# An attention and mixture-of-experts kernel: three key/value groups per turn instead of two, with other pacing of the side work

## The chip, the cores and the metric

One Trainium2 chip, all eight cores, one program launched on all of them. The metric is the device time of the slowest core in microseconds (us). Each core works alone on half of the tokens of one batch element; no data passes between cores.

## The reference, cut to what matters

```python
# x: (4, 4096, 1024) f32, 16 heads of 64
qkv = einsum('btc,fc->btf', x, w_qkv)
p = softplus(q @ k.T * hs**-0.5) ** 2 * causal
attn = p / (p.sum(-1) + 1e-9)
x = layernorm(x + (attn @ v) @ w_proj.T + b_proj)
probs = softmax(x @ router_w.T); topk_vals, topk_idx = top_k(probs, 2)
topk_w = topk_vals / (topk_vals.sum(-1) + 1e-6)
out = sum over the 2 experts of (x @ expert_weights[e] + probs[e]) * topk_w[e]
x = layernorm(x + out)
```

## The kernel before, in words

A core owns 2048 query rows in four slots of 512; for slot 0 to 3 it attends to 1024, 2048, 3072 and 4096 keys. Heads are taken in eight head pairs. First all queries are projected (`qall`). Then comes the attention part, the subject here, and then a tail.

**Steps.** The list `seq` has 16 entries, called steps 0 to 15 here (`si` in the code): steps 0 to 7 are the eight head pairs in pass 0 (slots 0 and 1), steps 8 to 15 the same head pairs in pass 1 (slots 2 and 3).

**Turns.** A step runs over pairs of 128-key blocks: 4 + 8 = 12 turns in a step of pass 0, 12 + 16 = 28 in one of pass 1, 320 in all. They are numbered from 0 within a step. In turn n the program issues, in this order:

1. TensorE: four score matmuls into `psS`, which is one set of four banks. They wait for the Exp of turn n-1, which reads it.
2. `pop_av` (L432): the probability-times-value matmuls (AV) of turn n-2. When that was the last turn of a slot, four VectorE copies take `psA` and `psB` out; that happens in turn 1 and in turn 5 (pass 0) or 13 (pass 1). After the last slot of a step, so in turn 1 of the next, `queue_epilogue` (L463) queues nine items.
3. Groups of the keys and values of the step after this (`kv_groups`, L287): 20 groups in four chunks of 512 tokens, each chunk one K group (8 matmuls of 512 columns) and four V groups (8 of 128 columns). Groups use the banks `psK` and `psV` in turn (`bg_bank`, L275), and each is copied out by VectorE before its bank is used again. Turn 0 of a step has no groups. The chunks' inputs lie in two buffers `xkb`: when the last V group of a chunk is issued, the load of the chunk after the next is put into GpSimd's queue (1 MB, `load_xk`). Once no group is left, the call that finds none issues what the step after the next one needs: its weights `wqK` (0.5 MB) and two `xkb` chunks (1 MB each).
4. One item of the epilogue `epi_q`: turn 1 adds 1e-9 (VectorE), turns 2 and 3 a reciprocal each (VectorE), turns 4 to 7 one store `scr` each (2 KB to HBM, GpSimd's queue), turns 8 and 9 one broadcast load `bcb` (two DMAs of 64 KB, GpSimd's queue) and the VectorE product `attn<-attn,bcb`. A `bcb` load waits for all four `scr` stores of the step; the product waits for `bcb`.
5. In pass 1, after the 72 epilogue items of pass 0, items of `work_q`: projection, layernorm, routing and expert matmuls for the first half of the rows. An item has a tag: 1 holds matmuls, 2 holds VectorE or ScalarE work, 0 neither. At most one item of tag 1 or 2 goes into a turn. Tag 0 are the expert weight loads (256 KB each, four to a half of an expert, GpSimd's queue), issued in the four turns before the half is needed. What is left of `work_q` goes to the tail.
6. ScalarE: Exp (`t_exp<-psS`) and Ln (`spb<-t_exp`). There is one `spb`, so Ln of turn n waits until VectorE has squared that of turn n-1.
7. VectorE: the square `pbb<-spb`, and in the last four turns of a slot the mask product `pbb<-pbb,mkb`.

Every engine runs its own instructions in the order of issue. All loads of `xkb`, `wqK` and expert weights, and `scr` and `bcb`, go through GpSimd's one DMA queue; SyncE's queue has the spill of keys and values to HBM (`kvs`, 1 MB after group 20 in pass 0) and the residual rows `stream` (4 MB, at the start of step 2, and 4 MB more in the tail).

In the profile every instruction has line 1066, that of the helper that emits it, so groups are told apart by tile names.

Of the kernel before, what the change touches and what calls it, by code (L numbers as in the profile page):

```python
# [24 lines left out]
PASS_SLOTS = {0: (0, 1), 1: (2, 3)}  # L25
# [39 lines left out]
def build_program(debug=DEBUG):  # L65
# [75 lines left out]
    with contextlib.ExitStack() as ctx:  # L141
# [52 lines left out]
        def load_wq_usage(k, guard_t):  # L194
            hp = k % 8
            qn = "WQ%d" % (k % 4 if k < 8 else k % 2)
            wts = [(sem["T"], guard_t)] if guard_t else []
            if k < 8:
                dst = wqA[k % 4]
                src = ap(d_wq8, hp * D * 384,  # L200
                         [[384, 128], [384 * 128, 8], [1, 384]])
            else:
                dst = wqK[k % 2]
                src = ap(d_wq8, hp * D * 384 + 128,
                         [[384, 128], [384 * 128, 8], [1, 256]])
            ld_wq[k] = (qn, emit("g", "dma_start", dst, src,
                                 w=wts, i=[(qn, 16)]))
# [10 lines left out]
        def load_xk(p, hp, tc):  # L218
            bi = tc % 2
            qn = "XB%d" % bi  # L220
            wts = [(sem["T"], xkb_guard[bi])] if xkb_guard[bi] else []
            xk_load[(p, hp, tc)] = (qn, emit(
                "g", "dma_start", xkb[bi],
                ap(d_xkf, 512 * tc, [[4096, 128], [4096 * 128, 8], [1, 512]]),
                w=wts, i=[(qn, 16)]))
# [178 lines left out]
        v_cool = [0]  # L404
# [483 lines left out]
        for si, (hp, p) in enumerate(seq):  # L888
# [19 lines left out]
            for slot in PASS_SLOTS[p]:  # L908
                npair = PAIRS[slot]
                for j in range(npair):  # L910
# [23 lines left out]
                    if len(av_queue) >= 2:  # L934
                        pop_av()
                    if not (slot == PASS_SLOTS[p][0] and j == 0):
                        for _ in range(2):
                            ng = next(kvq, None)
                            if ng is not None:
                                ng()  # L940
                            elif not kv_done[0]:
                                kv_done[0] = True
                                if si + 2 < len(seq):
                                    load_wq_usage(8 + si + 2,
                                                  kv_tlast[seq[si]])
                                    nhp, npp = seq[si + 2]
                                    for tc in ((0, 1) if npp == 0 else (4, 5)):
                                        if (npp, nhp, tc) not in xk_load:
                                            load_xk(npp, nhp, tc)
                    v_cool[0] = max(0, v_cool[0] - 1)  # L950
                    heavy_done = 0
                    pops = 0
                    if slot == PASS_SLOTS[p][1] and j >= npair - 1:
                        heavy_done = 1
                    if epi_q:
                        epi_q.pop(0)()
# [1 line left out]
                    while (work_q and pops < 3  # L958
                           and epi_pops[0] >= P0_EPI):
                        tag = work_q[0][0]  # L960
                        if tag == 1 and heavy_done:
                            break
                        if tag == 2 and (heavy_done or v_cool[0]):
                            break
                        fn = work_q.pop(0)[1]
                        fn()
                        pops += 1
                        if tag:
                            heavy_done = 1
                        if tag == 2:  # L970
                            v_cool[0] = 1
                    par = gpair[0] % 2
                    gpair[0] += 1
                    wexp = [(sem["T"], t_sc)]
# [173 lines left out]
```

How the kernel before makes its waits and increments, by code:

```python
            def run(eng):  # L1058
                for waits, method, args, kw, incs in recs[key]:
                    for s, val in waits:
                        if val:
                            eng.wait_ge(s, val)
                    if method == "wait_ge":
                        eng.wait_ge(*args)
                        continue
                    instr = getattr(eng, method)(*args, **kw)
                    for nm, n in incs:
                        instr.then_inc(sem[nm], n)
```

## Time and profile before

| | before |
|---|---|
| median of the runs | 2041.87 us (2 runs, 2040.83 to 2042.9) |
| the profiled execution | 2041.92 us; its slowest core's span 2040.2 us (core 3) |
| spans of the eight cores | 2009.8 to 2040.2 us |
| query projection, up to the first Exp | 0 to 140.5 us |
| steps 0 to 7 | 140.5 to 591.1 us |
| steps 8 to 15 | 591.1 to 1646 us |
| tail | 1646 to 2040 us |

Busy time of an engine over the whole span says little here, since the stages have different limits; what is read is how far apart the Exp activations of successive turns lie, and what ScalarE waited for in between.

### The profile page before, as it was taken

The page shows a single profiled execution, that of the slowest core. Times are in us where ns is not written, and L with a number is a line of the kernel's source. Part 1 is how long each engine was busy: PE and PEld are TensorE (multiplying, and loading weights), DVE is VectorE, ACT ScalarE, POOL GpSimd, SP SyncE. Part 2 cuts the span into 40 slices and gives each one's busy share as a digit, 9 for nine tenths or more (in the row PEclk, how much of TensorE's full clock was granted, in tenths as well). Part 3 has the DMA queues.
Part 4 walks back from the last instruction along what each step waited for, and adds up shares of the span by engine and source line. Part 5 has one row for each costly group of instructions (what it writes and reads, how often), then busy time and mean ns, then how long its engine had stood idle before and what let it go on. Part 6 is the DMA issues. An engine that isn't in the chain of part 4 may idle for free.

```text
span 2040.2 us, 26095 instructions; the slowest of 8 cores (2009.8 to 2040.2 us)
## 1 busy us (share of the span) xinstructions
PE 1456.4 (71%) x7968; PEld 638.4 (31%) x7968; DVE 1155.7 (57%) x1524; ACT 1234.5 (61%) x687; POOL 245.5 (12%) x362
## 2 busy tenths in 40 slices
PE   1967666666777785758887887688884436599991
PEld 0433333333333232323433333234331112344440
DVE  0026757777666666655666555456667437444446
ACT  0229867888887979969788696597897720000000
POOL 1000111111111010020110200201100001022110
PEclk9978887888898989889999999899996758599995
DMA  9888677876875033281471833714300023144542
GB/s 159 111 120 129 106 154 127 127 114 105 139 119 79 1 66 55 42 119 22 81 101 28 114 57 59 107 22 81 50 1 6 0 72 119 22 77 70 82 63 82
DMA packets 146384, 162.47 MB, mean 80 GB/s; under 512 B 8784, under 2 KB 135888, under 8 KB 146128
## 3 DMA queue, kind: packets, MB, share of 16 engines
q0 software_dynamic: 137328, 128.10, 44.1%
q1 hardware_dynamic: 8928, 32.71, 4.4%
q8 instruction: 75, 1.23, 0.2%
q14 instruction: 53, 0.43, 0.1%
HBM read 269.65 MB, written 16.97 MB: 140 GB/s over the span
## 4 chain that ended last, share of the span: by engine, by line
PE 32%; ACT 28%; DMA 17%; DVE 11%; issue 10%; POOL 1%; DVEq 1%; ACTq 0%; SPq 0%; POOLq 0%
ACT spb L1066 14%; ACT t_exp L1066 14%; PE psK L1066 13%; PE psV L1066 11%; DMA xkb<-xkf 6%; PE psS L1066 4%; DVE pbb L1066 3%; DMA qall<-ew 3%; PE psA L1066 2%; DMA bcb<-scr 2%; DMA xq<-xqf 2%; PE psB L1066 2%; DMA scr<-rsb 2%; DVE rsb L1066 2%; DVE stream L1066 2%
## 5 line engine op out<-in xcount | busy, mean ns | idle before, releaser
L1066 ACT ACTIVATE t_exp<-psS 128x2048 bf16<-128x2048 f32 x320 | 600.7, 1877 | 225.2 <-PE psS L1066 202.5
L1066 ACT ACTIVATE spb<-t_exp 128x2048 bf16<-128x2048 bf16 x320 | 611.2, 1910 | 83.9 <-DVE pbb L1066 41.7
L1066 DVE TENSOR_TENSOR pbb<-spb 128x2048 bf16<-128x2048 bf16 x320 | 390.1, 1219 | 270.8 <-ACT spb L1066 254.1
L1066 PE MATMUL psS<-qall,kb 64*128 64x512 bf16 x1280 | 211.4, 408 | 217.8 <-ACT t_exp L1066 195.9
L1066 PE MATMUL psA<-pbb,vb 128*65 128x512 bf16 x640 | 272.2, 425 | 78.4 <-DVE vb L1066 31.3
L1066 PE MATMUL psB<-pbb,vb 128*65 128x512 bf16 x640 | 268.8, 420 | 0.0
L1066 ACT ACTIVATE lnr<-lnv 128x4 f32<-128x4 f32 (+1 forms) x6 | 1.2, 206 | 365.0 <-DVE lnv L1066 365.0
L1066 DVE SCALAR_TENSOR_TENSOR stream<-psK,gates,stream 128x512 f32<-128x512 f32 x128 | 95.8, 748 | 144.2 <-PE psK L1066 143.8
L1066 PE MATMUL psK<-qall,h1fm 128*128 128x512 bf16 x512 | 128.0, 395 | 53.4 <-DMA qall<-ew 39.8
L1066 DVE TENSOR_TENSOR pbb<-pbb,mkb 128x2048 bf16<-128x2048 bf16 x128 | 156.8, 1225 | 13.4 <-DVE pbb L1066 0.2
L1066 PEld LDWEIGHTS psA<-pbb,vb 128*65 128x65 bf16 x640 | 74.5, 116 | 275.1 <-issue 246.4
L1066 DVE SCALAR_TENSOR_TENSOR stream<-psV,gates,stream 128x512 f32<-128x512 f32 x128 | 95.7, 748 | 103.6 <-PE psV L1066 103.2
L1066 PEld LDWEIGHTS psS<-qall,kb 64*128 64x128 bf16 x1280 | 43.2, 95 | 339.5 <-issue 337.2
L1066 POOL DMA_DIRECT2D xkb<-xkf x64 | 57.3, 897 | 745.2 <-PE psK L1066 438.2
L1066 PE MATMUL psV<-qall,h1fm 128*128 128x512 bf16 x512 | 124.0, 386 | 12.5 <-DVE kb L1066 6.7
L1066 PE MATMUL psK<-ewh,h1fm 128*128 128x512 bf16 x512 | 122.6, 383 | 6.4 <-DVE g_t L1066 6.4
L1066 PE MATMUL psV<-ewh,h1fm 128*128 128x512 bf16 x512 | 121.2, 380 | 0.0
L1066 DVE CAST kb<-psK 128x512 bf16<-128x512 f32 x32 | 22.1, 692 | 160.6 <-PE psK L1066 160.3
L1066 PE MATMUL psK<-xkb,wqK 128*128 128x512 bf16 x256 | 77.9, 459 | 31.4 <-DMA xkb<-xkf 22.6
L1066 PE MATMUL psS<-xq,wqA 128*128 128x512 bf16 x256 | 62.2, 407 | 45.5 <-DMA xq<-xqf 41.5
L1066 PEld LDWEIGHTS psB<-pbb,vb 128*65 128x65 bf16 x640 | 76.3, 119 | 40.5 <-issue 12.3
L1066 PEld LDWEIGHTS psK<-qall,h1fm 128*128 128x128 bf16 x512 | 50.2, 100 | 116.9 <-issue 64.8
(90 smaller groups left out, 1421.7 us busy)
## 6 DMA issues: line engine op xcount, KB each, us to landing
xkb<-xkf POOLq DMA_DIRECT2D x64, 1024.0 KB, 11.9
qall<-ew POOLq DMA_DIRECT2D x64, 256.0 KB, 7.3
ewh<-ew POOLq DMA_DIRECT2D x64, 256.0 KB, 6.0
wqK<-wq POOLq DMA_DIRECT2D x16, 512.0 KB, 8.3
stream<-xot SPq DMA_DIRECT2D x16, 512.0 KB, 11.4
wqA<-wq POOLq DMA_DIRECT2D x8, 768.0 KB, 20.9
out<-stream SPq DMA_DIRECT2D x12, 512.0 KB, 2.6
kvs<-vb SPq DMA_DIRECT2D x8, 520.0 KB, 11.0
```

Source lines behind the costliest of these rows:

```text
L1066: instr = getattr(eng, method)(*args, **kw)
```

## The change

Three constants in the loop over turns. Up to three groups are issued in a turn instead of two. The last two turns of a step, not only the last one, take no item of tag 1 or 2. After an item of tag 2 the counter `v_cool` is set to 2 instead of 1; it is lowered by one ahead of the test, so a 1 never held anything back, and a 2 holds back a tag 2 item (and what stands behind it) for one turn.

```diff
@@ -934,7 +934,7 @@
                     if len(av_queue) >= 2:
                         pop_av()
                     if not (slot == PASS_SLOTS[p][0] and j == 0):
-                        for _ in range(2):
+                        for _ in range(3):
                             ng = next(kvq, None)
                             if ng is not None:
                                 ng()
@@ -950,7 +950,7 @@
                     v_cool[0] = max(0, v_cool[0] - 1)
                     heavy_done = 0
                     pops = 0
-                    if slot == PASS_SLOTS[p][1] and j >= npair - 1:
+                    if slot == PASS_SLOTS[p][1] and j >= npair - 2:
                         heavy_done = 1
                     if epi_q:
                         epi_q.pop(0)()
@@ -968,7 +968,7 @@
                         if tag:
                             heavy_done = 1
                         if tag == 2:
-                            v_cool[0] = 1
+                            v_cool[0] = 2
                     par = gpair[0] % 2
                     gpair[0] += 1
                     wexp = [(sem["T"], t_sc)]
```

## Rows read from the trace of the kernel before

**Rows 1.** ScalarE's timeline, step 5: start, length, tile; in brackets idle time before.

```profile
426.18 1.88 ACT L1066 ACTIVATE t_exp<-psS 128x2048 bf16<-128x2048 f32 x1
430.21 1.88 ACT L1066 ACTIVATE t_exp<-psS 128x2048 bf16<-128x2048 f32 x1
438.59 1.88 ACT L1066 ACTIVATE t_exp<-psS 128x2048 bf16<-128x2048 f32 x1 [4.45 <-PE psS L1066]
...
464.56 1.88 ACT L1066 ACTIVATE t_exp<-psS 128x2048 bf16<-128x2048 f32 x1
...
480.66 1.88 ACT L1066 ACTIVATE t_exp<-psS 128x2048 bf16<-128x2048 f32 x1
```

**Rows 2.** The same in step 11: turns 1, 8 and 11.

```profile
977.19 1.88 ACT L1066 ACTIVATE t_exp<-psS 128x2048 bf16<-128x2048 f32 x1
...
1014.07 1.88 ACT L1066 ACTIVATE t_exp<-psS 128x2048 bf16<-128x2048 f32 x1 [0.47 <-PE psS L1066]
...
1030.74 1.88 ACT L1066 ACTIVATE t_exp<-psS 128x2048 bf16<-128x2048 f32 x1 [1.69 <-PE psS L1066]
```

**Rows 3.** VectorE's instructions of step 5, grouped: count, busy us, mean ns, idle before.

```profile
L1066 DVE TENSOR_TENSOR pbb<-spb 128x2048 bf16<-128x2048 bf16 x12 | 14.6, 1212 | 6.4 <-ACT spb L1066 6.4
L1066 DVE TENSOR_TENSOR pbb<-pbb,mkb 128x2048 bf16<-128x2048 bf16 x8 | 9.8, 1225 | 0.8
L1066 DVE RECIPROCAL rsb<-rsb 128x256 f32<-128x256 f32 x2 | 3.5, 1743 | 0.0
L1066 DVE CAST kb<-psK 128x512 bf16<-128x512 f32 x2 | 1.4, 692 | 4.1 <-PE psK L1066 4.1
L1066 DVE COPY rsb<-psB 1x512 f32<-1x512 f32 x2 | 1.4, 688 | 0.1
```

**Rows 4.** TensorE's timeline in turns 1 to 3 of step 5.

```profile
433.65 2.90 PE L1066 MATMUL psK<-xkb,wqK 128*128 128x512 bf16 x8 [3.56 <-DVE attn L1066]
...
442.30 0.61 PE L1066 MATMUL psK<-wqK,xkb 128*128 128x128 bf16 x8
442.75 1.89 PE L1066 MATMUL psV<-xkb,wqK 128*128 128x512 bf16 x8
```

**Rows 5.** GpSimd's timeline, step 5, turns 5 to 8: when its DMAs are issued.

```profile
452.82 0.92 POOL L1066 DMA_DIRECT2D xkb<-xkf  x1 [3.98 <-DVE attn L1066]
453.74 1.50 POOL L1066 DMA_DIRECT2D scr<-rsb  x3
462.70 0.53 POOL L1066 DMA_DIRECT2D bcb<-scr  x1 [7.45 <-DVE vb L1066]
```

**Rows 6.** DMA view, windows 452 to 456 us and 1526 to 1532 us: issue to landing.

```profile
xkb<-xkf POOLq DMA_DIRECT2D x1, 1024.0 KB, 8.7
scr<-rsb POOLq DMA_DIRECT2D x3, 2.0 KB, 7.2
...
scr<-rsb POOLq DMA_DIRECT2D x4, 2.0 KB, 1.6
```

**Rows 7.** DMA view of three issues at 469.9, 470.9 and 473.9 us.

```profile
wqK<-wq POOLq DMA_DIRECT2D x1, 512.0 KB, 7.9
...
xkb<-xkf POOLq DMA_DIRECT2D x1, 1024.0 KB, 17.2
...
xkb<-xkf POOLq DMA_DIRECT2D x1, 1024.0 KB, 19.2
```

**Rows 8.** DMA view, step 9: `wqK` issued at 765.4, `xkb` at 766.4 and 771.8.

```profile
xkb<-xkf POOLq DMA_DIRECT2D x2, 1024.0 KB, 14.6
```

**Rows 9.** Expert weights: the chain's longest wait for them; landing in an empty queue.

```profile
1296.35 20.30 DMA qall<-ew
...
qall<-ew POOLq DMA_DIRECT2D x4, 256.0 KB, 5.7
```

**Rows 10.** ScalarE's timeline, step 15: its wait at the first layernorm batch.

```profile
1561.16 0.21 ACT L1066 ACTIVATE lnr<-lnv 128x4 f32<-128x4 f32 x1 [6.98 <-DVE lnv L1066]
```

**Rows 11.** The chain that ended last, steps 1 and 2: one chunk's load.

```profile
240.56 34.69 DMA xkb<-xkf
```

## The prediction

> **What bounds the kernel now.** First the distance between Exps. ScalarE needs 4.03 us for Exp and Ln of a turn when nothing holds it [rows 1]: 320 turns are 1288 us. From the first Exp at 140.5 to 1646 the attention part took 1505, so some 217 us are turns in which something else ended last; the 394 us tail is another stage, in which the change moves little. Which turns these are is read from the Exp starts. In step 5, turn 1 took 8.38 us (430.21 to 438.59), turns 1 to 7 together 34.4, the whole step 54.5 where 48.3 is the floor [rows 1]. In step 11 turns 1 to 10 took 53.6 where 40.3 is the floor [rows 2]. So in pass 0 ScalarE binds almost everywhere; the turns with groups are the slow ones in pass 1, where TensorE carries groups and an expert half block together. Then the DMA view, for what small transfers do behind big ones: on that the sum turns.
>
> **Three groups, the turns themselves.** The 20 groups now end in turn 7 (18 by turn 6, then 2), not in turn 10. A K group costs TensorE 1.75 to 1.9 us, a V group 0.45 [rows 4]; no work is added, it is crowded into seven turns. With two banks, the third group of a turn needs the first one's copy, and VectorE comes to that only after the square and, in masked turns, the mask (1.21 + 1.23), in turns 1 and 5 also after four copies of 0.69, and it has the reciprocals (1.74) in turns 2 and 3 [rows 3]. Laid out by hand for step 5, from Exp to Exp:
>
> - Turn 1 (K V V): square and mask to 2.6, four copies to 5.4, K copy to 6.1, then the third group and the scores (0.6): 7.45. It was 8.38, of which 4.45 was idle time that ended with a late `xkb` [rows 1]; this wait goes, as the loads come four turns earlier.
> - Turns 2 to 7: 5.15, 5.5, 5.05, 5.1, 4.4, 4.03 (V V K and V V V behind mask and reciprocal, V K V, V V V behind the four copies, K V V, V V).
>
> Sum 36.7, against 34.4 before: +2.3, and turns 8 to 10 fall to the floor, where they nearly were. In pass 1, with an expert item as a fourth user of the two banks, the same laying out gives 8.0, 6.1, 5.05, 6.2, 4.65, 6.2, 4.4 = 40.6; with turns 8 to 10 at 4.03 it is 52.7, against 53.6 [rows 2]: a gain of 0.9. By itself, then, the crowding is about neutral.
>
> **Three groups, the moved loads.** What is issued when the groups end (`wqK`, two `xkb`, 2.5 MB) stood at turn 11, behind the epilogue. Now it stands in turn 7, in GpSimd's queue ahead of the fourth `scr` store and of both `bcb` loads. GpSimd issues in order and the second `xkb` waits for the last V group of turn 7, so `scr` is issued behind it; `bcb` waits for `scr`; the product waits for `bcb`; and it stands in VectorE's queue ahead of the square of turn 8, for which Ln of turn 9 waits on ScalarE. The question is how long a 2 KB store takes behind 2.5 MB. With the queue empty it takes 1.6 us; issued 1 us behind an `xkb` load it takes 7.2, landing with that load (8.7) [rows 5, 6]. It takes the load's place in time, so I let it land with the last load.
>
> When that is, for step 5 with Exp 1 at 430.2: Exp 4 at 448.3, Exp 7 at 462.9, Exp 9 due at 470.9 and Ln 9 at 472.9. The third chunk pair's load is issued at 449.5 and lands 8.7 later, 458.3 [rows 6]. `wqK` is behind it: 7.9 alone [rows 7], less about 1.9 that a transfer needs with nothing ahead (estimate from the 1.6 of `scr`, rows 6): 464.3. Then two `xkb`. Before, `wqK` landed at 477.8 and the second `xkb` at 493.1 [rows 7], 15.3 for two with the spill beside them, as it will be: 479.6. The second is issued at 464.2, so the queue, not the issue, decides. `scr` lands at 479.7, both `bcb` 4.7 later (before, `bcb` was issued at 462.7 [rows 5] and its product began some 5 us after), square done at 486.1. Ln 9 is 13.2 late; the second `bcb` adds about 1. A step of pass 0: 48.3 + 8.5 (turns 1 to 7 over the floor) + 14.2 = 71.0.
>
> There are seven such steps, 1 to 7. Step 0 has no epilogue: 54. The 4 MB of `stream` loads, behind which an `xkb` took 34.7 us [rows 11] instead of 19.2 [rows 7], fall into the stall of step 1: +15. Pass 0: 54 + 7 x 71 + 15 = 566 against 450.6, **+115**.
>
> Step 8 has the stall without expert work: **+14**. In steps 9 to 13 the turns 4 to 7 are longer (21.3 against 20.1) and no spill runs beside the loads: after `wqK` the two `xkb` need 13 [rows 8]. In step 11's times, Exp 4 at 996.4: third pair lands 1006.2, `wqK` 1012.2, second `xkb` 1025, square 1031.3 with the expert copy, Ln 9 due at 1023.9: 7.5, with the second `bcb` 8.7. Less the gain of 0.9, +7.8 each, 39; in steps 11 and 12 the 256 KB expert loads stand in front too, +8: **+47**. Step 14 loads nothing: **-3**.
>
> **The other two edits.** Counting items off turn by turn: 208 turns of pass 1 could take a heavy item, now 199; the wait after tag 2 costs 11 more where tag 2 items follow each other. Of 196 heavy items the last four (three layernorm statistics and their batch) slip into the tail, where VectorE idles at first but then is full: +6 (bounds 0 and the 12 that they need). In step 15 the statistics stood in every turn and put VectorE behind; ScalarE stood 6.98 us at the first batch [rows 10] and about 4 at the second. Every other turn VectorE keeps up, and one batch is left, about 3: -16. Together **-10**. The item order shifts by up to nine turns, so that other expert halves meet a queue full of loads. Before, five did (up to 20.3 us from issue to landing, 5.7 in an empty queue [rows 9]); by the new order three do, by less: **-26**.
>
> **Sum.** 115 + 14 + 47 - 3 - 10 - 26 = +137; on the profiled execution's 2041.92 that is 2179 us, and the median of the runs (2041.87) is the same.
>
> **The rivals.**
>
> *A, the small store is not held up.* If `scr` lands within about 2 us of its issue in turn 7 (until 466.5 in the example), the chain `bcb`, product, square makes Ln 9 and no stall arises. The stalls are 7 x 14.2 + 15 + 14 + 5 x 8.7 + 8 = 179 of the sum; without them 2000 us, faster by 2.1%, through the lost `xkb` wait of turn 1, the expert waits and step 15. For it: its 1.6 us; against it: 7.2 behind one load [rows 6], and 64 KB and 256 KB transfers that also grew. The Trainium skill ("DMA: Bandwidth & Descriptors", Queues, rings and completion order) says that descriptors of one ring are consumed in order but that completion is not first in, first out for DMAs of one issuer, which speaks for A; its section on the increment by 16 says that a GpSimd DMA posts on all 16 engines whatever its shape, so that it would pass every ring's backlog, which speaks against it. By the first rule alone it would be 2000, by both 2179; the trace has `scr` landing within a microsecond of the load ahead.
>
> *B, the stalls are half as long*, since the loads are issued earlier or the two `xkb` overlap more (the second needs only 5 us after the first in rows 7): 90 less, 2089, at the edge of 2%.
>
> *C, crowding costs more.* TensorE after a pause ran a K group in 2.90 against 1.89 us [rows 4]; a stall of ten microseconds a step makes such pauses. If all four K groups of 15 steps take the slow time and more with their copies, 1.7 each, it is +100: 2279.
>
> The Trainium skill ("TensorE: Matmul & The Clock Gate", HAM oscillation) says that waits on DMAs throw the array back to 1.2 GHz each time. It bears on C; the slow K group above is the trace's case of it.
>
> **How the numbers follow.** Forecast 0.73, A 0.08, B 0.08, C 0.11. The range from 2095 to 2245 leaves out A, B and the top of C. About 2% (41 us) is what a measurement tells from no change. Slower by over 2%: 0.87 (forecast, C, part of B); within: 0.08 (part of B and of A); faster: 0.05 (part of A). The point is 2179.
>
> **What would show it.** In steps 1 to 13 one Ln in turn 9 should wait 5 to 14 us, released by `pbb`, and `DVE attn <- DMA bcb<-scr` should be the longest new wait, some 130 to 180 us over 13 times; the fourth `scr` should take about 15 us in pass 0. Turn 1 should lose its idle 4.45. Groups should be gone after turn 7, step 15 should be 16 shorter. It would be wrong if the fourth `scr` lands in 2 us, or if the stall is hidden because VectorE reaches the product late anyway.

## The result and the profile after

| | before | after |
|---|---|---|
| median of the runs of this comparison | 2041.53 us (10 runs) | 2234.12 us (11 runs) |
| ratio | | 1.094, 95% interval 1.0922 to 1.0959 |
| profiled execution, span of the slowest core | 2040.2 us (core 3) | 2231.7 us (core 6) |
| steps 0 to 7 | 450.5 us | 583.2 us |
| steps 8 to 15 | 1054.5 us | 1106.7 us |
| tail | 394.6 us | 402.7 us |

The changed kernel is 9.4% slower. The forecast was 2179 us, slower, with a range of 2095 to 2245; the time lies inside it, near its upper end. Of the 192 us, 133 are in pass 0, 52 in pass 1, 8 in the tail. In some executions, whatever the kernel, the cores of one die run at a lower granted clock and take several per cent longer; the ratios leave these out, and rows are taken from cores that did not.

The groups of instructions whose waits grew most (busy us, mean ns, then the idle time before them and what ended it), first before, then after.

```profile
L1066 ACT ACTIVATE t_exp<-psS 128x2048 bf16<-128x2048 f32 x320 | 600.7, 1877 | 225.2 <-PE psS L1066 202.5
L1066 ACT ACTIVATE spb<-t_exp 128x2048 bf16<-128x2048 bf16 x320 | 611.2, 1910 | 83.9 <-DVE pbb L1066 41.7
...
L1066 DVE TENSOR_TENSOR attn<-attn,bcb 128x512 bf16<-128x512 bf16 x32 | 13.5, 422 | 45.8 <-DMA bcb<-scr 45.7
```

```profile
L1066 ACT ACTIVATE t_exp<-psS 128x2048 bf16<-128x2048 f32 x320 | 600.7, 1877 | 299.0 <-PE psS L1066 278.5
L1066 ACT ACTIVATE spb<-t_exp 128x2048 bf16<-128x2048 bf16 x320 | 611.2, 1910 | 193.2 <-DVE pbb L1066 153.8
...
L1066 DVE TENSOR_TENSOR attn<-attn,bcb 128x512 bf16<-128x512 bf16 x32 | 13.6, 424 | 193.4 <-DMA bcb<-scr 193.4
```

ScalarE's work is the same. It idles in two ways. Ahead of Exp (`t_exp`) it waits for TensorE's scores, 278.5 us where it was 202.5: turns that are too full. Ahead of Ln (`spb`) it waits for VectorE's square, 153.8 us where it was 41.7: the stall. VectorE's 193.4 us of waiting for `bcb` were 45.7.

What TensorE's groups of keys and values waited for, from the first Exp to the last (the view of the tile `wqK`: us in total, times), first before, then after:

```profile
DMA xkb<-xkf: 27.8, 9
```

```profile
DVE vb L1066: 59.8, 36
DVE kb L1066: 45.3, 28
DMA xkb<-xkf: 36.7, 15
```

`vb` and `kb` are VectorE's copies of earlier groups, which have to empty a bank before the next group may use it. With two groups a turn no wait of a group ended with one of them; with three such waits add up to 105 us.

Step 5 again, the step that the prediction laid out. ScalarE's timeline: the Exp of turns 1, 8 and 9, the Ln of turn 9, and the first Exp of step 6.

```profile
512.18 1.88 ACT L1066 ACTIVATE t_exp<-psS 128x2048 bf16<-128x2048 f32 x1
...
554.62 1.88 ACT L1066 ACTIVATE t_exp<-psS 128x2048 bf16<-128x2048 f32 x1
...
558.64 1.88 ACT L1066 ACTIVATE t_exp<-psS 128x2048 bf16<-128x2048 f32 x1
570.00 1.91 ACT L1066 ACTIVATE spb<-t_exp 128x2048 bf16<-128x2048 bf16 x1 [9.48 <-DVE pbb L1066]
...
580.29 1.88 ACT L1066 ACTIVATE t_exp<-psS 128x2048 bf16<-128x2048 f32 x1
```

Exp 1 is at 512.18 and Exp 8 at 554.62: turns 1 to 7 took 42.4 us, where before had 34.4 [rows 1] and the prediction 36.7. Ln 9 waited 9.48 us, where the prediction had 13.2. The whole step took 72.1 us (508.15 to 580.29) against the 71.0 forecast.

What VectorE did in the stall (its timeline), and when GpSimd issued what it waited for (GpSimd's timeline), same step:

```profile
554.70 1.23 DVE L1066 TENSOR_TENSOR pbb<-spb 128x2048 bf16<-128x2048 bf16 x1 [1.92 <-ACT spb L1066]
568.35 0.43 DVE L1066 TENSOR_TENSOR attn<-attn,bcb 128x512 bf16<-128x512 bf16 x1 [12.43 <-DMA bcb<-scr]
568.69 1.22 DVE L1066 TENSOR_TENSOR pbb<-spb 128x2048 bf16<-128x2048 bf16 x1
```

```profile
534.56 0.90 POOL L1066 DMA_DIRECT2D xkb<-xkf  x1 [11.62 <-PE psV L1066]
535.56 1.61 POOL L1066 DMA_DIRECT2D scr<-rsb  x3
537.21 0.93 POOL L1066 DMA_DIRECT2D wqK<-wq  x1
543.00 0.89 POOL L1066 DMA_DIRECT2D xkb<-xkf  x1 [4.87 <-PE psK L1066]
552.85 0.88 POOL L1066 DMA_DIRECT2D xkb<-xkf  x1 [8.96 <-PE psV L1066]
553.73 0.52 POOL L1066 DMA_DIRECT2D scr<-rsb  x1
565.12 1.06 POOL L1066 DMA_DIRECT2D bcb<-scr  x2 [10.88 <-DMA scr<-rsb]
```

The DMA view of the issues between 552.8 and 554 us: the last `xkb` and the fourth `scr`, us from issue to landing.

```profile
xkb<-xkf POOLq DMA_DIRECT2D x1, 1024.0 KB, 11.5
...
scr<-rsb POOLq DMA_DIRECT2D x1, 2.0 KB, 10.8
```

The chain is the one foreseen: the last `xkb` load is issued when turn 7's last group is done, the 2 KB store 0.9 us behind it lands with it 10.8 us later, GpSimd waits for it (10.88), `bcb` takes 3 more, and VectorE stands 12.43 us before a product of 0.43 us, with the square of turn 8 behind it.

TensorE's timeline of the crowded turns of step 5, those rows at which a group waited:

```profile
518.43 0.61 PE L1066 MATMUL psK<-wqK,xkb 128*128 128x128 bf16 x8 [2.64 <-DVE kb L1066]
...
522.91 1.89 PE L1066 MATMUL psV<-xkb,wqK 128*128 128x512 bf16 x7 [1.46 <-DVE vb L1066]
...
530.08 0.61 PE L1066 MATMUL psK<-wqK,xkb 128*128 128x128 bf16 x8 [2.87 <-DVE vb L1066]
...
541.41 1.01 PE L1066 MATMUL psK<-wqK,xkb 128*128 128x128 bf16 x8 [2.55 <-DVE vb L1066]
...
546.61 1.67 PE L1066 MATMUL psV<-xkb,wqK 128*128 128x512 bf16 x7 [1.58 <-DMA xkb<-xkf]
```

Each is the third group of its turn, held by a VectorE copy, but for the last one, the first group of turn 6: there the chunk's load had not landed. (A wait of 0.57 us of the third group of turn 6 is left out.) The third group of turn 5 also ran slowly, 1.01 us where the same work took 0.61 in turn 1; the granted clock between 541.4 and 545.1 us was 0.56, near the lower of its two levels, after the pause of 2.55 us.

### The profile page after: what moved, and what is told of

It reads as the page before. It is cut to its first block, busy times and chain, and to the rows that moved or that the text cites. A ratio compares the mean times of both kernels' runs of the same rounds, so it can differ in the third digit from the quotient of the medians.

```text
span 2231.7 us, 25968 instructions; the slowest of 8 cores (2205.1 to 2231.7 us)
## 1 busy us (share of the span) xinstructions
PE 1495.8 (67%) x7841; PEld 647.3 (29%) x7968; DVE 1161.1 (52%) x1524; ACT 1234.7 (55%) x687; POOL 245.7 (11%) x362
## 4 chain that ended last, share of the span: by engine, by line
PE 30%; ACT 26%; DMA 22%; DVE 11%; issue 10%; POOL 1%; DVEq 1%; ACTq 0%; SPq 0%; POOLq 0%
ACT spb L1066 13%; ACT t_exp L1066 12%; PE psV L1066 12%; PE psK L1066 10%; DMA xkb<-xkf 8%; DMA scr<-rsb 6%; PE psS L1066 4%; DMA bcb<-scr 3%; DVE pbb L1066 3%; PE psA L1066 2%; DVE rsb L1066 2%; PE psB L1066 2%; DMA xq<-xqf 2%; DVE stream L1066 1%; DVE attn L1066 1%
## 5 line engine op out<-in xcount | busy, mean ns | idle before, releaser
L1066 ACT ACTIVATE t_exp<-psS 128x2048 bf16<-128x2048 f32 x320 | 600.7, 1877 | 299.0 <-PE psS L1066 278.5
L1066 ACT ACTIVATE spb<-t_exp 128x2048 bf16<-128x2048 bf16 x320 | 611.2, 1910 | 193.2 <-DVE pbb L1066 153.8
L1066 PE MATMUL psA<-pbb,vb 128*65 128x512 bf16 x640 | 289.8, 453 | 152.2 <-DVE pbb L1066 133.7
L1066 PE MATMUL psS<-qall,kb 64*128 64x512 bf16 x1280 | 223.1, 428 | 225.9 <-ACT t_exp L1066 206.0
L1066 PE MATMUL psB<-pbb,vb 128*65 128x512 bf16 x640 | 286.3, 447 | 0.0
L1066 DVE SCALAR_TENSOR_TENSOR stream<-psV,gates,stream 128x512 f32<-128x512 f32 x140 | 104.4, 745 | 130.0 <-PE psV L1066 130.0
L1066 PE MATMUL psV<-qall,h1fm 128*128 128x512 bf16 x581 | 154.8, 409 | 14.4 <-DMA qall<-ew 9.9
L1066 PE MATMUL psK<-wqK,xkb 128*128 128x128 bf16 x1096 | 89.6, 228 | 88.6 <-DVE vb L1066 47.3
L1066 DVE SCALAR_TENSOR_TENSOR stream<-psK,gates,stream 128x512 f32<-128x512 f32 x116 | 86.9, 749 | 84.0 <-PE psK L1066 83.3
L1066 DVE TENSOR_TENSOR attn<-attn,bcb 128x512 bf16<-128x512 bf16 x32 | 13.6, 424 | 193.4 <-DMA bcb<-scr 193.4
L1066 PEld LDWEIGHTS psK<-wqK,xkb 128*128 128x128 bf16 x1096 | 73.8, 102 | 113.7 <-issue 98.5
L1066 PE MATMUL psK<-qall,h1fm 128*128 128x512 bf16 x399 | 96.4, 379 | 5.1 <-DVE g_t L1066 3.2
## 6 DMA issues: line engine op xcount, KB each, us to landing
xkb<-xkf POOLq DMA_DIRECT2D x64, 1024.0 KB, 11.5
```

Source lines behind the costliest of these rows:

```text
L1066: instr = getattr(eng, method)(*args, **kw)
```

## The experiments

The theory after the result had two parts. The loads in turn 7 stall turn 9 (T1), and the third group of a turn waits for VectorE (T2). The rivals: one of the two carries nearly everything, or the pacing edits do harm. All ratios are to runs of the kernel before on the same chip, with a 95% interval in brackets; a time in us behind a ratio is that ratio times 2041.5. A difference of two ratios is uncertain by both of their intervals, and a difference under 2% is not counted as a change of a kernel by itself.

**The parts of the change alone.** `e1_groups3` has the group edit, `e2_pacing` the two others.

```diff
# e1_groups3, against before
-                        for _ in range(2):
+                        for _ in range(3):
# e2_pacing, against after
-                        for _ in range(3):
+                        for _ in range(2):
```

> The kernel before with three groups per turn alone, the other two edits left out. Theory (all of the loss is the group edit; the other two give about 14 us in step 15 and cost about 8 in the tail): 2225 to 2260 us. Rival (the pacing edits carry a part of the loss, through the order in which expert halves meet a full queue): 2200 us or less.

Measured 1.0973 (1.0915 to 1.103), 2240 us, as the theory had it.

> Two groups per turn, with the two pacing edits alone. Theory: step 15 about 14 us shorter, tail about 8 longer, expert waits moved by up to 20 either way: 2010 to 2045 us. Rival (the pacing edits cost by themselves): above 2060 us.

Measured 0.9902 (0.987 to 0.9933), 2021 us. The pacing edits cost nothing (1% less time, under the 2%), and the loss is the group edit's. Step 15 took 120.0 us in the profile of `e2_pacing`, 134.0 before.

**The loads back in turn 11.** `e3_late_loads` keeps all three edits and moves nothing but the issue of the last three loads.

```diff
# against after
-                            elif not kv_done[0]:
+                            elif not kv_done[0] and (
+                                    slot != PASS_SLOTS[p][0]) * PAIRS[PASS_SLOTS[p][0]] + j >= 11:
```

> The changed kernel, but wqK and the two xkb loads of the step after the next are issued in turn 11 as before, behind the epilogue; the groups still end in turn 7. Theory (the stall at turn 9 comes from loads ahead of the fourth scr store): the turn 9 excess of steps 1 to 13, 139 us summed in the changed kernel, goes, some 10 to 30 us of late xkb in turn 1 come back: 2100 to 2130 us. Rival (crowding three groups costs nearly all): 2180 us or more. Turns 1 to 7 of step 5 stay near 42 us by both.

Measured 1.0268 (1.0197 to 1.034), 2096 us, just under the expected range: 138 of the 213 us between 2021 and 2234 are where the loads stand, give or take some 16. Turn by turn it is nearly the same. The turns with the stall (turn 9 of steps 1 to 8 and 10 to 13, turn 7 of step 9) were 139 us over the floor in the changed kernel; here 10 are left, in steps 8 and 9. What ScalarE and VectorE waited for in this kernel (in total, times, longest), then what the groups waited for here and in `e2_pacing`:

```profile
ACT t_exp L1067 <- PE psS L1067: 271.5, 96, 31.0
ACT spb L1067 <- DVE pbb L1067: 31.9, 34, 3.3
DVE attn L1067 <- DMA bcb<-scr: 31.6, 14, 9.1
```

```profile
DVE vb L1067: 62.4, 41
DVE kb L1067: 42.0, 28
DMA xkb<-xkf: 25.5, 13
```

```profile
DMA xkb<-xkf: 31.6, 8
DVE vb L1066: 1.7, 1
```

The waits for `bcb` fell from 193.4 to 31.6 and those of Ln from 153.8 to 31.9, while Exp still waits 271.5 for its scores: T1 is gone, the crowding is whole. Crowding alone is the distance from `e2_pacing`, 1.0268 - 0.9902, or 75 us, again give or take some 16. The two kernels differ in the third group, and in their groups' waits by VectorE's copies: 104 us against 2. In the profiles 48 of the distance are in pass 0 and 28 in pass 1. Of the latter a part comes from the order in which expert halves meet loads: TensorE waited 28 us for expert weights in `e3_late_loads` and 13 in `e2_pacing`.

**The stall without the third group.** `e4_late_epilogue` is the kernel before; only its epilogue starts four turns later.

```diff
+                    turn = j + (PAIRS[PASS_SLOTS[p][0]] if slot != PASS_SLOTS[p][0] else 0)
-                    if epi_q:
+                    if epi_q and not (len(epi_q) == 9 and turn < 5):
```

> The kernel before, two groups per turn, but the nine epilogue items of a step start four turns later, so that the fourth scr store falls into turn 11, behind wqK and the two xkb loads, as it does in turn 7 of the changed kernel. No third group. Theory (the order of loads and scr alone makes a stall of 8 to 14 us in each of 13 steps): 2150 to 2210 us, with the stall in turn 1 of the next step. Rival (the stall needs the crowded turns): under 2085 us.

Measured 1.0343 (1.0288 to 1.0399), 2111 us: between the two, so the theory's size was wrong. The stall is there in pass 0, in turn 1 of the next step. DMA view of the issues from 496 to 506 us, and ScalarE's timeline in that turn:

```profile
xkb<-xkf POOLq DMA_DIRECT2D x2, 1024.0 KB, 18.7
wqK<-wq POOLq DMA_DIRECT2D x1, 512.0 KB, 8.4
scr<-rsb POOLq DMA_DIRECT2D x4, 2.0 KB, 1.6
```

```profile
515.33 1.88 ACT L1068 ACTIVATE t_exp<-psS 128x2048 bf16<-128x2048 f32 x1
529.08 1.91 ACT L1068 ACTIVATE spb<-t_exp 128x2048 bf16<-128x2048 bf16 x1 [11.88 <-DVE pbb L1068]
```

(1.6 is the median of four: the first three took that, the fourth, behind the loads, 18.) In pass 1 it is smaller: turn 13 took 5.7 to 9.7 us in steps 10 to 13, and 15.0 in step 8, whose turns are at the floor; in step 9 it does not show. In this kernel the last group stands in turn 10 and the fourth `scr` in turn 11, where both are in turn 7 in the changed kernel; turns with groups and an expert item are 5.6 us long, and no spill is in flight. In step 13 the last `xkb` landed 8.7 us after its issue, and Ln waited only 1.8 us. So the order alone makes the stall, without a third group, but its length is what the last load takes less the turns that lie between. The expectation took one geometry for both passes; that was wrong.

**Is it the store, or every small transfer?** `e12_scr_first` is the changed kernel with the fourth `scr` ahead of the loads; `bcb` stays behind them.

```diff
+                    if turn == 7 and epi_q:
+                        epi_q.pop(0)()        # ahead of the groups of turn 7
# (cut: the reckoning of turn; the later place takes no item in turn 7)
```

> The changed kernel, but in turn 7 the fourth scr store is issued ahead of the groups and so ahead of the second and, where GpSimd gets that far, of all three loads; the bcb loads still stand behind them. Theory (every small transfer on this queue waits for the loads ahead of it, bcb as well as scr): scr lands early but bcb lands with the last load, so the stall at turn 9 shrinks only by the 3 to 4 us of the second transfer, to about 6 where it was 9.4 over the floor: 2180 to 2215 us. Rival (the scr store alone was the trouble): the stall is gone, 2130 or less.

Measured 1.0752 (1.0715 to 1.0789), 2195 us, in the theory's range. The rows are of core 4. GpSimd's timeline, and the DMA view of the issues at 532 to 534 us:

```profile
514.76 0.97 POOL L1071 DMA_DIRECT2D scr<-rsb  x2
...
521.79 0.89 POOL L1071 DMA_DIRECT2D xkb<-xkf  x1 [5.13 <-PE psS L1071]
532.35 0.87 POOL L1071 DMA_DIRECT2D xkb<-xkf  x1 [9.67 <-PE psV L1071]
533.22 1.09 POOL L1071 DMA_DIRECT2D bcb<-scr  x2
```

```profile
xkb<-xkf POOLq DMA_DIRECT2D x1, 1024.0 KB, 12.9
...
bcb<-scr POOLq DMA_DIRECT2D x2, 64.0 KB, 11.7
```

The store is out of the way, and `bcb`, which takes 2.5 us alone, takes 11.7: it lands with the load it follows. Turn 9 of steps 3 to 7 took 11.0 us on average against 13.1 in the changed kernel. Of the two small transfers, whichever stands behind the loads is late.

**What the crowding consists of.** Both kernels here leave out the mask product of VectorE (`if j >= npair - 4:` made `if False:`): three groups with late loads (`e8_late_loads_nomask`) against two (`e9_pacing_nomask`).

> Three groups per turn with late loads and the pacing edits, and the mask product left out everywhere (part of the computation is missing: keys after the query count). To be compared with e9, two groups per turn and the same left out. Theory (the third group waits for VectorE's queue, in which the mask stands): crowding costs 30 to 50 us here, where it cost 76 with the masks; so e8 is 30 to 50 above e9. Rival (TensorE's own load or its slow clock is the cost): e8 stays 70 or more above e9.

> Two groups per turn with the pacing edits and the mask product left out everywhere (the same part missing as in e8). By both theories 5 to 30 us under the 2021 of the same kernel with masks: 1990 to 2015.

Measured 1.0131 (1.0058 to 1.0204) and 0.9795 (0.9775 to 0.9814). The distance is 0.034, 69 us (give or take some 15), almost the 75 with masks: the expected 30 to 50 were a miss. What the groups waited for in `e8_late_loads_nomask` says why it does not speak against T2:

```profile
DMA xkb<-xkf: 41.7, 14
DVE kb L1067: 39.5, 30
DVE vb L1067: 38.2, 27
```

They still waited 78 us for VectorE's copies, where it was 104 with masks and nothing in `e9_pacing_nomask`. The mask was only a quarter of what the third group stands behind; the square, the reciprocals and the copies of a finished slot are still there. A second limit shows in the turns. In step 4, turns 2 and 3 fell from 5.5 and 5.9 us (`e3_late_loads`) to 4.5 and 5.0, but turn 4 rose from 5.5 to 10.6. TensorE's timeline of `e8_late_loads_nomask` there:

```profile
409.84 0.61 PE L1067 MATMUL psK<-wqK,xkb 128*128 128x128 bf16 x8 [1.53 <-DVE vb L1067]
...
416.60 3.57 PE L1067 MATMUL psK<-xkb,wqK 128*128 128x512 bf16 x8 [4.19 <-DMA xkb<-xkf]
```

The chunk is needed before it has landed, and after that pause its K group ran in 3.57 us instead of 1.89, at a granted clock of 0.50 (the lower level, 1.2 GHz) from 416 to 420.2 us. So `e10_nomask_norefill` also leaves out the loads of the third and fourth chunk.

```diff
-                            if tc + 2 in tcs:
-                                load_xk(p, hp, tc + 2)
-                qx, vx = xk_load[(p, hp, tc)]
+                qx, vx = xk_load[(p, hp, tcs[tc % 2])]
# (two places; the lines of e8_late_loads_nomask are cut)
```

> The kernel of e8 (three groups, late loads, no mask), and the third and fourth xkb chunk of a step are not loaded: their groups read the first two again (part of the computation is missing: masks, and half of the keys and values are wrong). Theory (with the mask gone, turns 4 and 6 wait for an xkb load that is issued in turn 2 or 4 and takes 9 to 12 us, so crowding has two limits, VectorE's queue and the refill of xkb): against e8 turn 4 of steps 3 to 7 falls from 8 to 10 to about 5, 2020 to 2050 us. Rival (the rest is TensorE's slow clock and load): 2060 or more.

Measured 0.9888 (0.9828 to 0.9948), 2019 us. Turn 4 of steps 3 to 7 took 4.1 to 4.4 us, and against `e9_pacing_nomask` 0.0093 is left, 19 us, give or take some 13. That kernel also spares other waits for `xkb` and bandwidth, so 19 us is a lower bound of what the rest of the crowding costs. The profiles say where: in pass 0 it is still 33 us above `e9_pacing_nomask` (43 with the refill), in pass 1 it is 4 below (29 above with the refill), and there two expert halves that TensorE had waited for in `e8_late_loads_nomask` came in time, 16 us. Its groups still waited 78 us for VectorE's copies. So crowding has two limits side by side. The third group waits for VectorE's queue; and five groups in 1.7 turns use up a chunk faster than the next one lands, which binds more when the groups come sooner. By the waits the first is the larger. How the 75 us divide between them is not shown.

**The other way.** If crowding costs, spreading should gain. `e6_early_wq` moves only the load of `wqK` to turn 0; `e7_all` goes down to one group per turn in pass 1 as well and has the pacing edits; `e11_spread` repairs two things that `e7_all` showed.

```diff
# e7_all, against before (cut to the lines that add)
+                    if slot == PASS_SLOTS[p][0] and j == 0 and si + 2 < len(seq):
+                        load_wq_usage(8 + si + 2, kv_tlast[seq[si]])   # was behind the last group
-                        for _ in range(2):
+                        for _ in range(2 if p == 0 else 1):
# and the two pacing edits. e11_spread, against e7_all
# step 0: wqK again behind the last group; the eight stream tiles:
-            if si == 2:
-                for t_ in range(8):
+            if 3 <= si <= 6:
+                for t_ in range(2 * si - 6, 2 * si - 4):
```

> The kernel before, but wqK of the step after the next is loaded in turn 0 of a step instead of turn 11, where only the two xkb loads stay. Theory (what waits in turn 1 is an xkb that lands behind wqK, 17 us after its issue, and would land in 9): turn 1 of steps 3 to 7 falls by 2 to 4 us, expert waits behind the loads by some 5 each: 2005 to 2030 us. Rival (the copies of the finished slot in VectorE's queue hold turn 1 anyway): 2035 to 2045.

Measured 0.9975 (0.9956 to 0.9994), 2036 us: the rival's range. Turn 1 of steps 3 to 7 did fall, from between 7.6 and 9.2 us to between 4.0 and 6.8, but turn 2 rose from 4.0 to as much as 5.8, because the square, behind the four copies of the finished slot, now is what is late (in step 7 Ln waits 1.96 us for it); and in step 0 turn 1 took 19 us, since there `wqK` stood ahead of the first `xkb`.

> The opposite of crowding: two groups per turn in pass 0, one per turn in pass 1 (20 of 28 turns), wqK loaded in turn 0, and the two pacing edits. Theory (in pass 1 a turn with one group and an expert item nearly fits under ScalarE's 4.03 us, so turns 1 to 10, 13 us over the floor before, cost 5 to 6 over turns 1 to 20): 1930 to 1975 us. Rival (spreading only moves the same cost to more turns): 1995 or more.

Measured 0.9616 (0.9594 to 0.9637), 1963 us, in the theory's range and 58 us under `e2_pacing`.

> The kernel of e7 with two repairs: in step 0 wqK stays behind the xkb loads, and the eight residual tiles are loaded two a step in steps 3 to 6 instead of all at the start of step 2. Theory: turn 1 of step 0 falls from 20 to about 8, the late xkb of step 2 (16.9 in one turn) goes: 1930 to 1950 us. Rival (other waits take their place): 1955 or more.

Measured 0.9502 (0.9469 to 0.9536), 1940 us: 5% faster than the kernel before and 294 us faster than the changed one. In pass 1 the turns with groups are at or near the floor; what is left is in single turns, expert halves behind an `xkb` load (up to 11.6 us in a turn) and the layernorm batches. The waits of Exp for its scores, 202.5 us in the kernel before (in total, times, longest):

```profile
ACT t_exp L1069 <- PE psS L1069: 93.3, 37, 31.3
```

## Why the prediction was right, and where its terms were off

- **The mechanism.** The stall stood where it was put: in turn 9, Ln released by `pbb` after 6.8 to 10.6 us (21.2 in step 1), in each of steps 1 to 8 and 10 to 13 (turns of 10.6 to 18.2 us, 25.0 in step 1); in step 9 it shows as a turn of 17.6 two turns earlier, at the layernorm batch that waits for the same VectorE queue. `DVE attn <- DMA bcb` grew by 148 us over before, in the 130 to 180 foreseen. Rival A is refuted by three runs: `scr` 10.8 us behind a load, the stall gone in `e3_late_loads`, and `bcb` 11.7 us in `e12_scr_first`. Of the two rules of the Trainium skill ("DMA: Bandwidth & Descriptors") weighed there, the one on the increment by 16, which a GpSimd DMA posts on all 16 engines, fits what was seen. The other, in Queues, rings and completion order, is told there of the queues of SyncE and ScalarE; that completion is not strictly in order showed on GpSimd's too, in that a `scr` store landed up to 1.5 us before the load ahead of it (544.7 against 546.2 in step 5), which changed nothing.
- **The size of the stall: 13.2 forecast, 9.5 measured in step 5.** Two terms. The turns before it were longer than laid out, and that time drained the queue: `wqK` and the first `xkb` had landed by 555.0, so only the last load's own 11.5 us counted, not a backlog of 15.4. The fourth `scr` took 8.1 to 11.5 us in steps 2 to 7, where about 15 was forecast. And the product came 4.7 us after the landing of `scr` in the sum, 3.8 in the trace (564.5 to 568.35). In step 1, with the 4 MB of `stream` beside it, turn 9 took 25.0 us; that is 12 more than in step 5, where 15 was forecast. Rival B, stalls of half the length (90), is about as far from the 138 measured as the forecast's 179.
- **"By itself the crowding is about neutral": the step that failed.** It was put at +2.3 us a step in pass 0 and -0.9 in pass 1. Its waits for VectorE were the right ones, but turns 1 to 6 were all sized too short: turns 1 to 7 took 42.4 instead of 36.7 in step 5, and 48.0 instead of 40.6 in step 11 (before: 34.4 and 36.9 [rows 1, 2]). `e3_late_loads` against `e2_pacing` gives 75 us for it. Of the 5.7 us in step 5, 2.6 are in turn 6 (7.0 for 4.4), 1.3 in turn 5 (6.4 for 5.1), the rest in turns 1 to 4. The hand layout left out two things. One is the `xkb` refill: it let the load of turn 4 take 8.7 us; with `wqK` issued 2.7 us behind it, it took 11.6, and turn 6 waited 1.58; in step 11, with expert loads in the queue too, turn 6 took 11.4 for 6.2. The other is TensorE's clock after a pause: behind the wait of 2.55 us in turn 5 the third group took 1.01 us for 0.61 and the scores 1.04 for 0.61. And the time that turns 8 to 10 give back is small, since in pass 0 they were near the floor already.
- **The expert waits: -26 forecast, -31 found.** Turns that wait for an expert half lost 46 us before (five of them in steps 10 to 14) and 14.5 after: turn 17 of step 10 (5.6 us), turn 5 of step 12 (12.1) and turn 3 of step 13 (10.7), the three that were counted off. Steps 9 to 13 grew by 49 us all the same, where 21 were forecast: their turns 1 to 7 grew by 53, where the layout gave 18 (3.7 each), and 14 of the 53 are the stall of step 9, which stands in turn 7.
- **The small terms held.** Step 15: -16 forecast, -14 measured. Tail: +6 and +8. Step 14: -3 and -2.
- **Rival C** had the right sign, more than laid out for crowding, but not by the cause it gave. It had all 60 K groups slow. In the trace of the kernel before 13 of them took over 2.5 us, in that of the changed kernel 6 (at most 11, since the first matmul of 47 groups is missing from this trace), in `e2_pacing` 10 and in `e3_late_loads` 8 by the same count. The granted clock did fall, from 0.885 to 0.844 for the slowest core, and other matmuls slowed: from `e2_pacing` to `e3_late_loads` TensorE's busy time in the attention part rose from 1076 to 1103 us for the same instructions. How much of these 27 us lies on ScalarE's path was not measured.
- **Two readings** in the prediction are off, and nothing hangs on them: by its own lists turns 4 to 7 are 21.5 us against 18.6 (not 21.3 against 20.1), and by the code 207 turns of pass 1 could take a heavy item, not 208.

In sum: the stalls were forecast at 179 and measured at 138; the crowding at -6 (137, less 179, plus the 36 of the two next terms) and measured at 75; pacing and expert order at -36, where `e2_pacing`, with an order of its own, measured -20. The stalls were put 41 us too high and the crowding 81 too low, so that 2179 came within 55 us of the time is in part luck; the direction and the stall are not.

## What to carry to other kernels

Here the time of a small transfer was set by what stood ahead of it in its queue. Before moving a large load earlier, look for small transfers that come to stand behind it, and follow each to the in-order engine that waits for it. When work is packed into fewer turns, check every buffer it passes (here two banks and two chunk buffers) for its refill time; a total that still fits says nothing about the turn. Where one engine sets a floor per turn, try spreading the side work thinly over all turns before finishing it early: here `e7_all`, with one group a turn in pass 1, was 58 us faster than `e2_pacing`.

## What the runs showed that was not expected

- A 1 MB load is slowed by what is issued after it. In steps 1 to 6 of the changed kernel the `xkb` load of turn 2, with nothing behind it, took 8.6 to 8.8 us, and the one of turn 4, with three `scr` and the 0.5 MB `wqK` behind it, 11.6 to 12.2. In `e3_late_loads`, where `wqK` comes later, the load of turn 4 took 8.5 to 9.3 in steps 2 to 6. So the queue is first in, first out only roughly.
- A 2 KB store takes 1.6 us with the queue empty, 7 to 12 us close behind one load and 18 us behind three (step 5 of `e4_late_epilogue`); a 64 KB load takes 2.5 alone and 11.7 behind a load. Behind loads, the small transfer's own size hardly matters.
